# Windowed attention and a routed feed-forward layer: TensorE's groups in another order within each half-slot

## The reference

```python
def _L0_attn_ref(x, Wq, Wk, Wv, Wo):            # x: layernorm of the input
    q, k, v = split_heads(x @ Wq), split_heads(x @ Wk), split_heads(x @ Wv)
    k_win, v_win = jnp.take(k, idx, axis=2), jnp.take(v, idx, axis=2)   # the last 64 tokens
    scores = jnp.einsum('bhld,bhlwd->bhlw', q, k_win) * scale
    scores = jnp.where(invalid[None, None, :, :], -jnp.inf, scores)
    attn = jax.nn.softmax(scores, axis=-1)
    ctx = jnp.einsum('bhlw,bhlwd->bhld', attn, v_win)
    return ctx.transpose(0, 2, 1, 3).reshape(Bx, Lx, D_OUT) @ Wo
...
x = x + _L0_attn_ref(_layernorm(x, axis=-1), Wq, Wk, Wv, Wo)
x = x + _L0_ffn_ref(_layernorm(x, axis=-1), w_router, w1, w2, bias)     # top 2 of 8, capacity 2048
```

## Time and profile before

| | us |
|---|---|
| three runs | 927.88, 932.2, 918.02; median 927.88 |
| profiled execution | 919.62 |
| its span in the profile | 917.8 |

### The profile page before, as it was taken

The page is one execution under the profiler, slowest core; times in us unless marked ns, Lnnn a source line. Parts: engine busy times, 40 slices in busy tenths (PEclk is TensorE's granted clock), DMA queues, the critical chain, the costliest instruction groups (busy, mean ns, idle before and its releaser), DMA issues.

```text
span 917.8 us, 19142 instructions
## 1 busy us (share of the span) xinstructions
PE 786.6 (86%) x7456; PEld 545.4 (59%) x7458; DVE 518.2 (56%) x1559; ACT 437.9 (48%) x884; POOL 353.7 (39%) x317
## 2 busy tenths in 40 slices
PE   8999999999999999999999998500999789789880
PEld 3455556556556556556556555400899689778770
DVE  3887877888887887887877886420122112121210
ACT  3556585485585574575575563000444344233320
POOL 2000000022222222222222224355287778778777
PEclk9999999999999998999999998555899999999995
DMA  2951100010010010010011011113145445454433
GB/s 75 368 200 32 34 8 13 13 42 29 26 47 28 20 53 28 20 50 32 20 50 32 20 53 36 58 42 105 35 60 104 80 79 85 78 103 62 79 33 33
DMA packets 48579, 54.21 MB, mean 59 GB/s; under 512 B 6002, under 2 KB 37385, under 8 KB 47473
## 3 DMA queue, kind: packets, MB, share of 16 engines
q0 software_dynamic: 22528, 17.22, 12.7%
q1 hardware_dynamic: 25968, 35.86, 11.7%
HBM read 17.70 MB, written 31.59 MB: 54 GB/s over the span
## 4 chain that ended last, share of the span: by engine, by line
PE 44%; DVE 22%; issue 15%; POOL 12%; DMA 5%; SPq 1%; POOLq 0%; ACT 0%; DVEq 0%
POOL out L431 10%; PE sT_ps L1061 9%; DVE kmax L652 5%; PE u_ps L1086 5%; PE tail_ps L1070 4%; PE sT_ps L1276 3%; PE sT_ps L1078 3%; PE sT_ps L1055 3%; DMA out<-y_sb,xg 2%; DMA x_sb<-in_L_attn_x 2%; DVE ctx_sb L678 2%; PE o_ps L1095 2%; DVE moving L666 2%; PE tail_ps L1106 2%; PE tail_ps L1119 2%
## 5 line engine op out<-in xcount | busy, mean ns | idle before, releaser
L431 POOL DMA_INDIRECT out<-y_sb,xg x128 | 198.2, 1549 | 81.1 <-DVE y_sb L996 42.0
L349 POOL DMA_INDIRECT slots_dram<-send_rows,slot_id x112 | 110.0, 982 | 181.0 <-PE sT_ps L1078 148.0
L503 ACT ACTIVATE probsT<-sT_ps 128x1024 f32<-128x1024 f32 x128 | 131.2, 1025 | 81.8 <-PE sT_ps L1078 78.2
L652 DVE TRANSPOSE_TENSOR_REDUCE kmax<-sT_ps 128x32 f32<-128x1024 f32 x128 | 159.6, 1247 | 17.7 <-PE sT_ps L1061 12.7
L1061 PE MATMUL sT_ps<-qbd,kT 32*128 32x256 f32 x1024 | 146.8, 404 | 0.0
L584 ACT ACTIVATE hT<-sT_ps 128x512 f32<-128x512 f32 x128 | 76.5, 598 | 141.8 <-PE sT_ps L1276 133.8
L364 POOL TENSOR_TENSOR xbias<-x_sb,bias_sb 128x256 f32<-128x256 f32 x32 | 23.3, 729 | 286.8 <-PE sT_ps L1078 279.9
L1276 PE MATMUL sT_ps<-xT_hl,w_hl 128*128 128x512 f32 x384 | 103.4, 421 | 17.6 <-DVE xT_hl L983 17.6
L1061 PEld LDWEIGHTS sT_ps<-qbd,kT 32*128 32x128 f32 x1024 | 88.3, 186 | 35.7 <-issue 29.3
L1276 PEld LDWEIGHTS sT_ps<-xT_hl,w_hl 128*128 128x128 f32 x384 | 74.7, 202 | 34.4 <-issue 12.5
L1086 PE MATMUL u_ps<-probsT,v_sb 128*32 128x128 f32 x2048 | 84.1, 283 | 0.0
(11 more groups left out here) (134 smaller groups left out, 1111.3 us busy)
## 6 DMA issues: line engine op xcount, KB each, us to landing
slots_dram<-empty_rows SPq DMA_DIRECT2D x8, 1096.0 KB, 14.8
xg<-slots_dram SPq DMA_DIRECT2D x32, 274.0 KB, 2.9
out<-xbias SPq DMA_DIRECT2D x32, 128.0 KB
w_sb<-in_L_ffn_w SPq DMA_DIRECT2D x16, 256.0 KB
send_rows<-rows_sb SPq DMA_DIRECT2D x7, 548.0 KB, 3.1
out<-y_sb,xg POOLq DMA_INDIRECT x128
slots_dram<-send_rows,slot_id POOLq DMA_INDIRECT x112
out<-empty_rows SPq DMA_DIRECT2D x1, 1024.0 KB, 20.0
```

The costliest lines, as they stand in the source:

```text
L349: pool.indirect_dma_start(out=slots_dram, out_offset=bass.IndirectOffsetOnAxis(ap=slot_id[:, k, j:j + 1].bitcast(U32), axis=0), in_=rows[: ...
L431: pool.indirect_dma_start(out=out, out_offset=bass.IndirectOffsetOnAxis(ap=xg[:, r, 4 * c + k, ROW - 1:ROW].bitcast(U32), axis=0), in_=y_s ...
L503: nc.scalar.activation(probsT[:, gp].rearrange("p b k h q -> p (b k h q)"), sT_ps[:, gp].rearrange("p b c -> p (b c)"), ACT.Exp).then_inc( ...
L652: nc.vector.tensor_reduce(kmax[:, u % 2, :], sT_ps[:, u % 2].rearrange("p b (c q) -> p (b c) q", q=32), AX.X, ALU.max, apply_transpose=Tru ...
```

## The change

TensorE and ScalarE get another order within a half-slot; no instruction of computation is added or taken out. On TensorE the groups that use the whole array stand together behind shifted, then the strips of columns, then the groups by rows. The first half is now: shifted, context_T of tile g - 2, query_key (t odd) or values (t even), at t = 5 normed_again_T, at t = 6 the router, project of g - 2, weighted, maxima_T, fill. The second half: shifted, weighted_T, normed_T (t even), at t = 5 the router, weighted, maxima_T, fill, at t = 4 normed_again_T. context_T of a tile moves from the end of a second half to the half-slot behind it, in front of the project of the same tile. values moves from the second half of slot t - 1 to the first half of slot t, where it is wanted in the second; normed_T moves from the first half to the second.

ScalarE follows: the copy of context_T comes ahead of the first exponential, values in the first half (t even), the copy of normed_T behind the second exponential. The wait of TensorE for the row maximum (s_negmax) ahead of context_T is gone, as shifted has already waited for what comes behind it.

```diff
--- before.py
+++ after.py
@@ -523,29 +523,31 @@
                 g = b * TILES + t
                 if t == 5 and not first:
                     normed_again_T(b, 0)
+                if not (first and t < 2):
+                    context_T(g - 2)
                 exps(g, 0)
                 if t == 7 and not first:
                     gate_exps(b - 1)
+                if t == 5 and not first:
+                    normed_again_T(b, 1)
                 if not (first and t == 0):
                     weighted_out(g - 1)
-                if t % 2 == 0 and (t < 4 or not last):
-                    normed_T(b * PAIRS + (t + 4) // 2, (t + 4) // 2 % PAIRS)
+                if t % 2 == 0 and not (first and t == 0):
+                    values(b * PAIRS + t // 2, t // 2)
                 if t % 2 == 1 and (t < 5 or not last):
                     query_key(b * PAIRS + (t + 3) // 2, (t + 3) // 2 % PAIRS)
                 if t == 4 and not first:
                     normed_again(b, 0)
-                if t == 5 and not first:
-                    normed_again_T(b, 1)
                 exps(g, 1)
+                if t % 2 == 0 and (t < 4 or not last):
+                    normed_T(b * PAIRS + (t + 4) // 2, (t + 4) // 2 % PAIRS)
                 if t == 4 and not first:
                     normed_again(b, 1)
-                if t % 2 == 1 and (t < 7 or not last):
-                    values(b * PAIRS + (t + 1) // 2, (t + 1) // 2 % PAIRS)
                 if t == 0 or t in (4, 6) and not last:
                     normed(b * PAIRS + (t + 6) // 2)
                 if t == 3 and not last:
                     normed(b * PAIRS + 4)
-                if not (first and t == 0):
+                if last and t == TILES - 1:
                     context_T(g - 1)
 
             normed(0)
@@ -1135,10 +1137,21 @@
                 ahead = t + 1 < TILES or not last
                 done, left = not (first and t == 0), not (first and t < 2)
 
+
+
                 shifted(2 * g)
-                if done:
-                    pe.wait_ge(s_exp, 2 * g)
-                    weighted((t - 1) % TILES, 1)
+                if left:
+                    pe.wait_ge(s_ctx, g - 1)
+                    context_T(g - 2)
+                if t % 2 == 1 and (t < 5 or not last):
+                    query_key(b * PAIRS + (t + 3) // 2, (t + 3) // 2 % PAIRS)
+                if t % 2 == 0 and left:
+                    n = b * PAIRS + t // 2
+                    pe.wait_ge(s_k_sb, min(n + 2, NPAIR))
+                    values(n, t // 2)
+                if t == 5 and not first:
+                    pe.wait_ge(s_xn2T_sb, 2 * (b - 1) + 1)
+                    normed_again_T(b, 1)
                 if left:
                     pe.wait_ge(s_ctxT_sb, g - 1)
                     if t == 6 and not first:
@@ -1146,13 +1159,9 @@
                     if t == 1 and b > 1:
                         counts(b - 2).then_inc(s_pos, 1)
                     project(g - 2)
-                if t % 2 == 1 and (t < 5 or not last):
-                    query_key(b * PAIRS + (t + 3) // 2, (t + 3) // 2 % PAIRS)
-                if t % 2 == 0 and (t < 4 or not last):
-                    n = b * PAIRS + (t + 4) // 2
-                    pe.wait_ge(s_v_sb, n - 1)
-                    pe.wait_ge(s_k_sb, n)
-                    normed_T(n, (t + 4) // 2 % PAIRS)
+                if done:
+                    pe.wait_ge(s_exp, 2 * g)
+                    weighted((t - 1) % TILES, 1)
 
                 if left:
                     pe.wait_ge(s_x2, g - 1)
@@ -1166,41 +1175,36 @@
                     if t % 2 == 1:
                         pe.wait_ge(s_k_sb, b * PAIRS + (t + 1) // 2 + 1)
                     fill((t + 1) % TILES, 0)
-                if t == 5 and not first:
-                    pe.wait_ge(s_xn2T_sb, 2 * (b - 1) + 1)
-                    normed_again_T(b, 1)
 
                 shifted(2 * g + 1)
-                if t % 2 == 0:
-                    pe.wait_ge(s_v_sb, b * PAIRS + t // 2 + 1)
-                if done:
-                    pe.wait_ge(s_u, g)
-                weighted(t, 0)
                 if done:
                     if left:
                         pe.wait_ge(s_ctx, g - 1)
                     if t == 5 and not first:
                         pe.wait_ge(s_xn2T_sb, 2 * b)
                     weighted_T(g - 1)
+                if t % 2 == 0 and (t < 4 or not last):
+                    n = b * PAIRS + (t + 4) // 2
+                    pe.wait_ge(s_v_sb, n - 1)
+                    pe.wait_ge(s_k_sb, n)
+                    normed_T(n, (t + 4) // 2 % PAIRS)
+                if t == 5 and not first:
+                    router(b, range(0, 4))
+                if t % 2 == 0:
+                    pe.wait_ge(s_v_sb, b * PAIRS + t // 2 + 1)
+                if done:
+                    pe.wait_ge(s_u, g)
+                weighted(t, 0)
                 if ahead:
                     maxima_T(2 * g + 2)
-                if t % 2 == 1 and (t < 7 or not last):
-                    n = b * PAIRS + (t + 1) // 2
-                    if t < 5 or not last:
-                        pe.wait_ge(s_k_sb, n + 2)
-                    values(n, (t + 1) // 2 % PAIRS)
-                if ahead:
                     pe.wait_ge(s_exp, 2 * g + 2)
                     fill((t + 1) % TILES, 1)
-                if done:
-                    if ahead:
-                        pe.wait_ge(s_negmax, 2 * g + 3)
+                if t == 4 and not first:
                     pe.wait_ge(s_ctx, g)
-                    if t == 5 and not first:
-                        router(b, range(0, 4))
+                    normed_again_T(b, 0)
+                if not ahead:
+                    pe.wait_ge(s_ctx, g)
                     context_T(g - 1)
-                if t == 4 and not first:
-                    normed_again_T(b, 0)
 
             def fill_zeros(n):
```

## The result

The changed kernel takes 952.6 us (median of four runs, 946.4 to 960.9) against 928.4 before (918.0 to 932.2): ratio 1.028, 95% interval 1.015 to 1.040. So it is slower, and whether by more than 2% this interval leaves open. The prediction said 937, between 908 and 957, and gave "slower by over 2%" a chance of 0.32. The profiled execution took 952.5.

The account below looks back on a forecast made before the run. It took latency chains, TensorE or VectorE to bound, depending on the half-slot. Terms of +1.9, +1.15, -1.9 and +0.6 gave +1.75 us a sequence, +13.5 over eight: 933 profiled or 941 from the median, stated 937, range 908 to 957.

Parts of the forecast that it names:

- my own case: Slower by the summed steps, stated as 937 us, own range 921 to 951; chance 0.52.
- (a): TensorE's array: 7 fewer shape changes per pair of slots, 0.14 us each, counting only where TensorE binds.
- The first rival: TensorE binds after all and shape changes count in full: 888, 868 or about 900 us; chance 0.15.
- my sum: Steps (b) to (e) together: +1.75 us a sequence, +13.5 us over eight.
- (b): First halves, even t: projection waits for context and ScalarE's copy, shifted at 4.04 us; +0.47 each, +1.9 a sequence.
- (c): First halves, odd t: context, queries and keys precede projection, shifted at 4.35 instead of 3.98; +0.36, sum +1.15.
- (d): Second halves, odd t: values and context leave, shifted at 4.12 instead of 4.46; -0.34, -1.3 at t = 5, sum -1.9.
- (e): Second halves, even t: VectorE's, 4.27 us as before, 0; at t = 4 a late exponential costs +0.6.
- Rival 2: Context copy heading ScalarE's queue in first halves takes 0.3 us longer than its row: 943 to 951 us; chance 0.28.
- Rival 3: Idle TensorE in odd second halves brings one low-clock stretch per sequence, 16 us more: 949 to 957; chance 0.05.

Follow-up runs that it names:

- experiment 7: Experiment 1 plus two zero matmuls behind the context, weighted right behind shifted in second halves only; 963.8 us, ratio 1.046, not used because signals came late.
- experiment 3: Changed kernel plus matmuls of zeros in TensorE's idle time at the ends of second halves; 922.0 us, ratio 0.985; again 921.2 us, 1.004.
- experiment 1: Changed kernel with context_T and its copy back at the end of the second half; 906.2 us, ratio 0.968; again 905.0 us, 0.985.
- experiment 4: Experiment 1 with weighted right behind shifted again in both halves; 933.3 us, ratio 1.010.
- experiment 6: Experiment 1 plus two zero matmuls behind the context and ScalarE's queue at t = 4 spread; 963.3 us, ratio 1.043, not used because signals came late.

## Why the prediction was right or wrong

The direction and the range held, but the range by luck: my own case ran from 921 to 951, the 8 us that the order cost would have given about 932 by the same working, and most of the loss came from a rival that I gave 0.05.

- **(a) Changes of shape.** Right that they pay nothing where VectorE binds: 0.03 us each in second halves (experiment 7). The first rival, TensorE as the bound, fell: 7 changes fewer in a pair made none of the five sequences compared in experiment 3 shorter, and even with the context back the kernel takes 905, not 868 to 900. The rule of the Trainium skill that stood against my sum (a change of tiling mode drains the array) is neither shown nor refuted here: the load still idles 0.23 behind one in this trace, but regrouping did not pay in every half. What grouping does give, in experiment 1, is that weighted leaves the chain ahead of the projection (0.44 of the 0.58 in experiment 4).
- **(b) Even first halves.** Mechanism and size right: projection at 1.33, maxima at 2.21, 4.01 at t = 4. At t = 0 another 0.28 came from the slow cast. Experiment 1 takes the copy off the chain: 3.51 (426.98 to 430.49).
- **(c) Odd first halves.** Right, a little high: t = 3 takes 4.30 (268.58 to 272.88) where I had 4.35.
- **(d) Odd second halves.** The gain at t = 3 is smaller: 4.30 (272.88 to 277.18) against 4.12 forecast. I had taken VectorE's 3.93 from one sequence; here it has more steps. TensorE's groups came to 3.21, as forecast (3.2).
- **(e) Even second halves.** At t = 4 right, 4.78, and shown by experiment 6. What I left at 0 elsewhere had a side that I didn't look at: the context's time left these halves too. At t = 2 and 6 TensorE is busy for 76% (3.37 of 4.43 us at t = 2), where before it was 89%.
- **The sum.** 1.75 us a sequence forecast; the measured price of the order at full clock is 1.1 on average (experiment 3 against before). Part by part (b) to (e) it is +1.7, +1.1, -2.0 and +0.3 against +1.9, +1.15, -1.9 and +0.6. So the sum was too large by more than half, and +13.5 should have been about +8.
- **Rival 2** (the copy longer than its row) is wrong: the copy took 0.27 and its handshakes less than I had.
- **Rival 3, the clock,** is what made the rest of the 33 us in the profiled execution: 578.4 us of attention against 547.0 with zeros is 31 us of lost clock, and the kernel before loses some 6 as well (its 544.9 us against 547 less 8). Its mechanism was right: odd second halves leave TensorE idle for a fifth to a quarter of the time, I wrote, and it was a quarter. The failed step is its size. I allowed one stretch in each sequence, 2 us each, 16 in all, and gave that 0.05 without a reason. The profile has 15 stretches, 2.1 us each: the price of one was right, but there were nearly twice as many, 9 behind odd second halves and 5 behind even ones, which had become idle too. Its other half held: behind the router's groups, where two of the three falls of before begin, none is left in this profile. The Trainium skill, "TensorE: Matmul & The Clock Gate", section "A second HAM failure mode: psum-queue depth-cycling", tells of a kernel in which frequent short idle times between groups of matmuls let the clock swing between its two levels; this case's trace agrees (14 of 15 falls behind a half at 72 to 79%, with halves of 5.9 to 7.4 us in the fence above).

## What to carry to other kernels

When an edit takes work out of TensorE's stretches that another engine bounds, work out TensorE's busy share there after it, not only the time saved: here about 75% in most second halves cost 31 to 33 us, four times the price of the order itself, and matmuls of zeros got it back. Grouping matmuls by shape was worth 0.03 us a change where VectorE binds and at most some 0.07 in the first half taken apart in experiment 4; what counted was which group stood ahead of the one that another engine waits for. Keep a producer, its copy and its consumer a half-slot apart: context at the end of one half and projection in the next took 3.86 us in the first half of t = 3, against 4.30 with context, copy and projection all in that half.

## What the runs showed of the hardware

- In the changed kernel TensorE's clock fell to 1.2 GHz behind half-slots in which it was busy for 72 to 79% of the time, with no idle time there longer than about 1.2 us, and stayed at 2.4 GHz where zeros raised these shares to 84% or more. In the kernel before it fell three times: once behind a half at 84%, and twice in the first half of t = 6, right behind a half in which it was busy all the time (350 to 358, behind the router's matmuls of 8 columns). So the busy share alone doesn't decide it; by what else it goes stays open.
- The time of one kernel goes with its clock from run to run: the changed kernel's runs went from 946.4 us at a mean clock of 0.901 to 960.9 at 0.878, while the one with zeros stayed within 2 us, at 0.934 to 0.938.
- VectorE's cast of 128x32 took 0.18 us at the median and 0.46 at most, before and after. Each slow one (13 before, 6 after) lay beside an indirect DMA of GpSimd; 16 and 12 others that lay beside one too took 0.18, and none without one was slow. I did not test whether that is the cause.
- One set of runs had signals from TensorE reach ScalarE and VectorE late (0.6 and 1.15 us in the fence above) in half-slots with two indirect DMAs of GpSimd, for three kernels, and not for the kernel before with zeros, which ran in the same set. The same program had none of it in another set.
